# A decoder layer stack: the gates' four partial sums are transposed by TensorE and added by VectorE, in place of a product with a selecting table

## The reference

```
gate_in = jnp.concatenate((q, k, v), axis=-1)
ig = (gate_in @ igate_kernel + igate_bias)...
fg = (gate_in @ fgate_kernel + fgate_bias)...
...
log_f = jax.nn.log_sigmoid(fg)
cs = jnp.concatenate([jnp.zeros((1, 1), log_f.dtype), jnp.cumsum(log_f, axis=0)], axis=0)
log_d = jnp.where(jnp.tri(s, dtype=bool), (cs - cs.T)[1:, 1:] + ig.T, neg)
m = jnp.max(log_d, axis=-1, keepdims=True)
d = jnp.exp(log_d - m)
```

## Time and profile before

| | |
|---|---|
| median of three runs | 2569.34 us |
| profiled execution, its own time | 2565.48 us |
| its span | 2563.7 us |
| TensorE busy | 2275.3 us (89%) |
| VectorE busy | 1913.1 us (75%) |
| ScalarE busy | 1423.1 us (56%) |
| GpSimd busy | 702.9 us (27%) |
| granted TensorE clock, mean | 0.98 |

### The profile page before, as it was taken

How to read it: one execution, slowest core, us unless ns; L and a number is a source line. 1 busy time by engine, 2 the same in 40 slices (tenths; PEclk the granted TensorE clock), 3 DMA queues, 4 the chain that set the end, 5 groups by cost and what they waited for, 6 DMA issues and landing times.

```text
span 2563.7 us, 55641 instructions
## 1 busy us (share of the span) xinstructions
PE 2275.3 (89%) x20672; PEld 1853.5 (72%) x20672; DVE 1913.1 (75%) x4589; ACT 1423.1 (56%) x4586; POOL 702.9 (27%) x1066
## 2 busy tenths in 40 slices
PE   3879999999999999999999999999999999999964
PEld 3657777777777777777777777777777777777753
DVE  3568787777778777878777777877787877787853
ACT  3445665565565556565556565555656555656532
POOL 0122233222233222223322223322222332222321
PEclk9899999999999999999999999999999999999976
DMA  4010111111111111011111111111101111111111
GB/s 114 18 34 26 42 43 51 51 49 32 38 34 50 51 51 42 26 43 42 51 51 45 33 41 34 51 50 51 42 26 42 43 50 51 43 34 34 34 34 41
DMA packets 267472, 109.94 MB, mean 43 GB/s; under 512 B 215234, under 2 KB 248258, under 8 KB 267202
## 3 DMA queue, kind: packets, MB, share of 16 engines
q1 hardware_dynamic: 258498, 89.61, 14.0%
q10 hardware_dynamic: 8704, 16.78, 1.7%
HBM read 89.57 MB, written 16.78 MB: 41 GB/s over the span
## 4 chain that ended last, share of the span: by engine, by line
PE 46%; DVE 30%; ACT 10%; issue 10%; POOL 3%; SPq 1%; DMA 1%; POOLq 0%; DVEq 0%; ACTq 0%
PE ps_g L593 36%; PE ps_g L601 7%; ACT p_a L944 4%; DVE neg_max L1232 3%; PE ps_s L593 3%; DVE qk L1225 2%; DVE decay L1352 2%; DVE ctx_t L1383 2%; DVE x_tok L1288 2%; POOL qk_rot L1569 2%; DVE ctx_t L1381 2%; DVE ln_stat_b L1195 1%; DVE ln_stat_a L1195 1%; DVE f_max L1463 1%; ACT p_all L944 1%
## 5 line engine op out<-in xcount | busy, mean ns | idle before, releaser
L944 ACT ACTIVATE p_a<-ps_s,neg_max 128x128 f32<-128x128 f32 (+1 forms) x1024 | 415.2, 442 | 63.5 <-DVE neg_max L1232 63.5
L593 PE MATMUL ps_g<-x_t_hi,wqkv_hi 128*128 128x256 f32 x1024 | 302.2, 295 | 18.5 <-DVE p_t L1261 17.1
L593 PE MATMUL ps_g<-x_t_lo,wqkv_hi 128*128 128x256 f32 x1024 | 287.2, 280 | 0.0
L593 PE MATMUL ps_g<-x_t_hi,wqkv_lo 128*128 128x256 f32 x1024 | 287.2, 280 | 0.0
L1232 DVE TENSOR_REDUCE neg_max<-ps_s 128x2 f32<-128x256 f32 (+1 forms) x512 | 257.2, 543 | 5.0 <-PE ps_s L593 5.0
L1656 POOL TENSOR_SCALAR p_all<-p_all,f_rec,g_bc 128x256 f32<-128x256 f32 x256 | 152.3, 607 | 361.9 <-DVE f_rec L1471 361.9
L1569 POOL TENSOR_TENSOR qk_rot<-qk_rot,const 128x512 f32<-128x512 f32 x128 | 164.6, 1286 | 291.4 <-DVE qk_rot L1218 291.2
L944 ACT ACTIVATION_READ_ACCUMULATOR p_a<-ps_s,neg_max 128x1 f32 x1024 | 234.5, 229 | 0.0
L995 ACT COPY p_t<-ps_g 128x384 f32<-128x384 f32 x256 | 119.2, 479 | 196.4 <-PE ps_g L601 193.9
L601 PE MATMUL ps_g<-const,p_a 128*128 128x128 f32 x1536 | 223.2, 284 | 4.3 <-ACT p_t L995 1.4
L593 PEld LDWEIGHTS ps_g<-x_t_hi,wqkv_hi 128*128 128x128 f32 x1024 | 195.5, 191 | 31.5 <-DVE p_t L1261 23.2
(11 more groups left out here) (203 smaller groups left out, 6247.5 us busy)
## 6 DMA issues: line engine op xcount, KB each, us to landing
x_tok<-in_x SPq DMA_DIRECT2D x32, 512.0 KB, 3.6
ctx<-in_ctx SPq DMA_DIRECT2D x64, 256.0 KB, 3.4
p_all<-in_L_ffn_Wq SPq DMA_DIRECT2D x128, 128.0 KB, 2.6
pt_all<-in_L_ffn_Wk SPq DMA_DIRECT2D x128, 128.0 KB, 3.0
y_out<-in_L_ffn_Wv SPq DMA_DIRECT2D x128, 128.0 KB, 3.1
out<-y_out ACTq DMA_DIRECT2D x32, 512.0 KB, 2.8
x<-in_L_attn_Wqkv SPq DMA_DIRECT2D x2, 512.0 KB, 7.6
p_all<-in_L_attn_Wqkv SPq DMA_DIRECT2D x1, 512.0 KB, 4.1
```

The lines of the kernel that those rows point to most:

```text
L593: return nc.tensor.matmul(o, l, r, start=first, stop=last)
L944: return nc.scalar.activation(o, i, f, **kw)
```

## The change

The table `gate_sum` is dropped. The second piece becomes two plain transposes of `gate_parts`, 128 x 128 each, so the bank `gate` holds all four strips, 2 x 128 values for each token row in place of 2 x 8. VectorE reads the 8 meaningful values of each of the four strips out of the bank and adds the four (a reduction whose innermost stride is 32 words), and then adds the bias in SBUF as a second instruction. A new semaphore `gated` stands between the bias addition and `g_abs`.

```diff
-             "gate_sum": np.tile(np.eye(GATE_ROWS, 2 * HX, dtype=np.float32), (P // GATE_ROWS, 1))}
...
             for t in range(TT):
-                done = mm(o[:, t * 2 * HX:(t + 1) * 2 * HX], gate_parts[:, t * P:(t + 1) * P], c["gate_sum"], True, True)
+                done = tr(o[:, t * P:(t + 1) * P], gate_parts[:, t * P:(t + 1) * P], eye)
             done.then_inc(filled.sem)
...
             dve.wait_ge(*full[("gate",), b])
-            v.tensor_tensor(gate, bank[("gate",), b][:, 0:TT * 2 * HX].rearrange("p (t g) -> p t g", t=TT), gate_bias.unsqueeze(1).to_broadcast([P, TT, 2 * HX]), ALU.add).then_inc(dve_emptied.sem)
-            yield
+            strips = bank[("gate",), b][:, 0:T].rearrange("p (t k r) -> p t r k", t=TT, k=KT)
+            v.tensor_reduce(gate, strips[:, :, 0:2 * HX, :], AX.X, ALU.add).then_inc(dve_emptied.sem)
             dve.wait_ge(*empty[("gate",), b])
+            v.tensor_tensor(gate, gate, gate_bias.unsqueeze(1).to_broadcast([P, TT, 2 * HX]), ALU.add).then_inc(gated.sem)
+            yield
+            dve.wait_ge(*gated(b))
             v.scalar_tensor_tensor(g_abs, fg, -1.0, fg, ALU.mult, ALU.max).then_inc(g_abs_made.sem)
```

More of the change, by code:

```diff
@@ L100, in constants @@
     parts = {"cos": cos, "sin": sin, "eye": eye,
-             "upto": upto, "one": np.ones((P, 1), np.float32), "minus_pick": -np.tile(np.eye(LO_AT, HX, dtype=np.float32), (P // LO_AT, 1)),
-             "gate_sum": np.tile(np.eye(GATE_ROWS, 2 * HX, dtype=np.float32), (P // GATE_ROWS, 1))}
+             "upto": upto, "one": np.ones((P, 1), np.float32), "minus_pick": -np.tile(np.eye(LO_AT, HX, dtype=np.float32), (P // LO_AT, 1))}
     where, at = {}, 0
@@ L238, in build @@
     x1_made, x2_made, ln_shift, y_made = count("x1_made"), count("x2_made"), count("ln_shift_c"), count("y_made", TT)
+    gated = count("gated")
     g_abs_made, g_exped, g_lned, log_f_made, a_made, m_scanned, m_hi, m_split = (count(n) for n in ("g_abs_made", "g_exped", "g_lned", "log_f_made", "a_made", "m_scanned", "m_hi", "m_split"))
@@ L1312, in stage_b @@
             dve.wait_ge(*full[("gate",), b])
-            v.tensor_tensor(gate, bank[("gate",), b][:, 0:TT * 2 * HX].rearrange("p (t g) -> p t g", t=TT), gate_bias.unsqueeze(1).to_broadcast([P, TT, 2 * HX]), ALU.add).then_inc(dve_emptied.sem)
+            strips = bank[("gate",), b][:, 0:T].rearrange("p (t k r) -> p t r k", t=TT, k=KT)
+            v.tensor_reduce(gate, strips[:, :, 0:2 * HX, :], AX.X, ALU.add).then_inc(dve_emptied.sem)
+            dve.wait_ge(*empty[("gate",), b])
+            v.tensor_tensor(gate, gate, gate_bias.unsqueeze(1).to_broadcast([P, TT, 2 * HX]), ALU.add).then_inc(gated.sem)
             yield
-            dve.wait_ge(*empty[("gate",), b])
+            dve.wait_ge(*gated(b))
             v.scalar_tensor_tensor(g_abs, fg, -1.0, fg, ALU.mult, ALU.max).then_inc(g_abs_made.sem)
```

## The result

The changed kernel takes 2578.48 us (median of eight runs, 2576.94 to 2583.54); the kernel before, in eight runs, 2568.33 us. The ratio is 1.004, with a 95% interval of 1.0029 to 1.0051. So it is slower by 10.2 us, 0.4%; forecast were 2577.3 us and 8.0 us more. The profiled execution took 2577.76 us, 12.3 us more than that of before.

What follows compares the result with a forecast made beforehand. The prediction took the gates' chain over VectorE and ScalarE, for which TensorE waits, as the bound. Reduction 0.053 + bias 0.205 = 0.26 us a step, times 31 is 8.0 us: median from 2569.34 to 2577.3 us, range 2570 to 2582.

Steps and rivals of the forecast that it cites:

- What bounds the kernel: From the gates to TensorE's decay product the chain runs over VectorE and ScalarE; TensorE waits there, in 31 steps of 32.
- The reduction: VectorE's sum of 64 PSUM values replaces an addition of 152 ns: 205 ns, 53 ns more a step.
- the nearest row: VectorE's read of `h_raw`, 8 values at a stride of 129 words in SBUF: 167 ns, against 168 ns dense.
- The bias: VectorE's second, dependent instruction in SBUF, with the semaphore hand-over: 0.19 to 0.21 us, taken as 0.205 us a step.
- GpSimd's copy: Small copy of 0.18 us from 1316.94, forecast to miss the bias addition by 0.4 us; if it caught it, 2585 us.
- The step: Period from gates to gates, forecast 0.26 us longer in each of 31 steps.
- the sum: VectorE's 0.053 + 0.205 = 0.26 us a step, times 31 steps 8.0 us; full cost as summed, chance 0.68.
- I take nothing: TensorE's two transposes in place of the product may save 0.05 to 0.1 us a step, hidden by idle; counted as zero.
- a missed wait on GpSimd or in a bank: Sign to look for: a period grown by more than the gates' own delay would mean something moved there.
- absorption: Rival: slack between the gates and the same place in the next step hides the delay; 2571 us, chance 0.16.
- a gain by TensorE's shorter product: Rival: the chain goes over the values' product, VectorE's cost is hidden, 1.6 to 3.1 us gained; 2567 us, chance 0.04.
- the dear read: Rival: VectorE's strided PSUM read costs double, 0.33 us a step, 10.1 us, 2579.5 us; chance 0.12 with a dear addition.

Runs made afterwards that it cites:

- that part alone: Kernel before with the two transposes and VectorE's single addition reading only the first strip of four: 2570.7 us, ratio 1.0013.

## Why the prediction held, and where it fell short

What bounds the kernel: right. The gates lie on the chain in every step but the first, a delay on them goes through in full (7.3 us in 30 steps where the clock didn't fall), and the reverse holds too: 0.20 us less on VectorE gave 6.5 us.

The reduction: 205 ns forecast from two larger ones, 202 measured; the stride of 32 words costs nothing against stride 0, as the nearest row suggested. The Trainium skill's note ("SBUF — State Buffer", Door 1: The DMA port swizzle) names matmuls as what such reads of PSUM slow down, and for this VectorE read the 202 ns decide. The bias: 0.205 us forecast, 0.21 measured from start to start, and GpSimd's copy didn't touch it. The step: 0.26 us forecast, 0.24 measured. This term of the sum was right in kind and in size, 7.4 us for 8.0.

TensorE: "I take nothing" was the step that failed, in two ways. The transposes save 0.23 us a step and not 0.05 to 0.1; I took the 0.31 us of two transposes elsewhere, where the next instructions in the queue are others, and the idle became 1.52 us in place of the 1.3 forecast. And both the saving and VectorE's delay lengthen an idle of TensorE, which I priced at zero because idle time that waits for another engine costs nothing by itself. But the clock fell in every third step, and that is 5 to 6 us of the profiled execution. No term of the sum and no rival was about the clock. I had asked that a period grown by more than the gates' delay be looked for, but as a sign of a missed wait on GpSimd or in a bank, and it wasn't one; by the median step the period even grew by the gates' delay alone.

The rivals: absorption is refuted by the step's 0.24 us; a gain by TensorE's shorter product too, since that part alone makes the kernel slower (1.0002 to 1.0023); the dear read is refuted by the 202 ns. The rise, 10.2 us, is that of the dear read (10.1) and not that of the sum (8.0), for a reason that neither named. That the time came within 1.2 us of the forecast is in part luck: the kernel before measured 2568.33 us and not the 2569.34 that the forecast started from, and in the medians less of the falls' cost shows than in the profiled executions.

## What to carry to other kernels

Look at the chain, not the busy share: moving work from the engine that is busy for 89% to one busy for 75% made this kernel slower, because at that place the first waits for the second. A wait of the matmul engine isn't always free to lengthen: before adding a quarter of a microsecond to one of 1 us, check the granted clock by stretches, and after the change look for steps that are longer than their neighbours. If such a wait can't be shortened, putting filler work of the matmul engine in front of it may hold the clock, as the transposes issued three times did in the middle of the run, though the total then showed little of it.

## What the hardware did that I had not expected

TensorE's granted clock fell to 0.5, that is from 2.4 to 1.2 GHz, in full steps with a mean idle of 1.28 to 1.54 us before the running sum, and in none with one of 1.11 us or less, in ten kernels. Between the two nothing was measured. It fell in one step of three or four and not in all, at the same idle. One fall cost 0.5 to 0.7 us of a step's time; part of the slower work lay in waits, since the wait for the split maximum is missing in ten steps of the changed kernel. Two fp32 products with a table of 8 columns hold the queue as long as two with 128 columns (0.37 us for either pair), and two fp32 transposes of 128 columns hold it for 0.13 us against 0.36.
